# The state loops of four batches run back to back: batch ends and openings in pieces inside the loops

## The reference, cut to what matters

```
xz = x @ W_in.T;  u, z = split(xz)                  # 256 + 256 channels
uc = silu(conv3(u) + conv_b)                         # depthwise, along the tokens
proj = uc @ W_xproj.T;  B, C, dt = split(proj)       # 16, 16, 8
delta = softplus(dt @ W_dt.T + b_dt);  A = -exp(A_log)
h_t = exp(delta_t * A) * h_(t-1) + (delta_t * u_t) * B_t     # 16 states for each channel
y = sum_n(h * C) + uc * D
x = x + layernorm((y * silu(z)) @ W_out.T)
# experts: 8 of which the 2 best are weighted, and one shared, with gelu between two products
x = x + layernorm(sum_e combine_e * (gelu(x @ W1_e) @ W2_e) + shared(x))
```

## Time and profile before

| | us |
|---|---|
| median of 3 runs | 3171.16 (3161.33 to 3174.09) |
| profiled execution | 3168.89 |
| its span | 3166.6 |
| PE / DVE / ACT / POOL busy | 2388.2 / 2153.1 / 1719.2 / 1412.3 |
| granted PE clock, mean | 0.876 of full speed |

### The profile page before, as it was taken

How to read it: one execution, slowest core, us unless ns; L and a number is a source line. 1 busy time by engine, 2 the same in 40 slices (tenths; PEclk the granted TensorE clock), 3 DMA queues, 4 the chain that set the end, 5 groups by cost and what they waited for, 6 DMA issues and landing times.

```text
span 3166.6 us, 42245 instructions
## 1 busy us (share of the span) xinstructions
PE 2388.2 (75%) x15570; PEld 1726.5 (55%) x15570; DVE 2153.1 (68%) x3701; ACT 1719.2 (54%) x2617; POOL 1412.3 (45%) x1331
## 2 busy tenths in 40 slices
PE   3115772786377478699999999999999569876977
PEld 1003452354255356377777777776777446755675
DVE  3993897399569822588878887887888543355334
ACT  4213771675367233488877877787778323322332
POOL 0351143034204400256765676657656641564156
PEclk8556996799689789699999999999999879887988
DMA  3000000000000000100000000010000100000000
GB/s 99 0 0 0 1 1 0 1 1 1 0 0 1 1 1 6 49 21 21 21 21 21 21 21 21 21 31 21 21 22 10 41 1 1 1 13 2 1 1 14
DMA packets 32029, 42.02 MB, mean 13 GB/s; under 512 B 8897, under 2 KB 18130, under 8 KB 31442
## 3 DMA queue, kind: packets, MB, share of 16 engines
q1 hardware_dynamic: 31826, 39.34, 4.6%
HBM read 12.05 MB, written 2.10 MB: 4 GB/s over the span
## 4 chain that ended last, share of the span: by engine, by line
PE 46%; DVE 24%; issue 13%; POOL 10%; ACT 5%; SPq 1%; DMA 0%; POOLq 0%; DVEq 0%; ACTq 0%
PE ps L954 10%; PE ps L932 6%; PE ps L943 6%; PE ps L710 3%; DVE MA L1090 3%; DVE BIG L351 3%; PE ps L914 2%; PE ps L1723 2%; POOL MA L379 2%; DVE ps L340 2%; DVE BIG L340 2%; DVE lnb L265 2%; DVE acc L589 2%; PE ps L645 2%; PE ps L647 1%
## 5 line engine op out<-in xcount | busy, mean ns | idle before, releaser
L1090 DVE TENSOR_REDUCE MA<-ps 128x1 f32<-128x1024 f32 x512 | 623.4, 1221 | 192.9 <-PE ps L932 180.1
L379 POOL TENSOR_TENSOR MA<-MA,BIG 128x1024 f32<-128x1024 f32 x120 | 279.9, 2355 | 630.2 <-DVE BIG L351 630.2
L954 PE MATMUL ps<-MA,WB 128*64 128x128 f32 x4096 | 504.4, 277 | 0.0
L954 PEld LDWEIGHTS ps<-MA,WB 128*64 128x64 f32 x4096 | 442.6, 137 | 88.4 <-issue 87.4
L932 PE MATMUL ps<-BIG 96*128 96x512 f16 x1024 | 314.5, 389 | 13.4 <-ACT WB L1017 5.0
L710 PEld LDWEIGHTS ps<-WB,HR 128*128 128x128 f32 x2304 | 297.2, 204 | 26.5 <-issue 8.9
L1017 ACT ACTIVATE WB<-ps,MA 128x1024 f32<-128x1024 f32 x206 | 229.7, 1115 | 149.8 <-DVE MA L1090 149.8
L710 PE MATMUL ps<-WB,HR 128*128 128x128 f32 x2304 | 305.0, 289 | 0.0
L632 ACT ACTIVATE HR<-ps,b 128x512 f32<-128x512 f32 x288 | 190.8, 687 | 147.5 <-PE ps L647 146.7
L1024 ACT ACTIVATE MA<-ps 128x1024 f32<-128x1024 f32 x256 | 259.9, 1015 | 4.9 <-PE ps L943 4.9
L497 PE MATMUL ps<-bc,sel 96*128 96x512 bf16 x256 | 92.4, 451 | 198.5 <-DVE BIG L351 99.0
(11 more groups left out here) (291 smaller groups left out, 5310.9 us busy)
## 6 DMA issues: line engine op xcount, KB each, us to landing
BIG<-BIG SPq DMA_DIRECT2D x192, 64.0 KB, 2.0
BIG<-WB SPq DMA_DIRECT2D x192, 64.0 KB, 2.0
WB<-w_dram SPq DMA_DIRECT2D x1, 2304.0 KB, 14.5
X<-x_dram SPq DMA_DIRECT2D x4, 512.0 KB, 12.5
HR<-w_dram SPq DMA_DIRECT2D x1, 2048.0 KB, 9.3
out_dram<-X SPq DMA_DIRECT2D x4, 512.0 KB, 3.2
WB<-wqkv_dram SPq DMA_DIRECT2D x1, 1536.0 KB, 6.3
WB<-w_dram SPq DMA_DIRECT2D x2, 512.0 KB, 8.8
```

The source lines that it names most:

```text
L379: e.tensor_tensor(yy[:, c, :], yy[:, c, :], db[n % 2][c], ALU.add).then_inc(*p_my.up(b, n, c))
L954: x = e.matmul(bank[6][64 * pp:64 * pp + 64, 0:128], V[(4 * b + g) % 2][:, k, 64 * pp:64 * pp + 64], DT[n % 2][:, 128 * k:128 * k + 128], ...
L1090: e.tensor_reduce(L_of(n)[:, c:c + 1], ps[s][:, :], AX, ALU.max, negate=True).then_inc(*v_amx.up(n, s))
```

## The change

The opening of batch b+1, the end of batch b-1 and the experts of batch b-1 are given due times inside the loop of batch b, in slots of 14 between the states. For that:

- `up` is doubled, and delta is kept in it; `dl` as a tile of its own goes. The parts of the B and C rows get two buffers (`rows`), so that those of the next batch are made while this batch's are read. `du`, `uc`, `xT[0]` stay single.
- Everything of openings and ends that went through `ps[0]` and `ps[1]` goes through bank 7, in pieces of 512 tokens, one after another: two transposes, four products for u, two for `wx`, four for `wdt`, four for z, two for the output. Each piece waits until the copy of the piece before it has left the bank (`to`). For batch 0, banks 0, 1, 2, 3 and 7 are taken by turns.
- The down product of the experts has bank 6 alone in batches 0 to 2, and banks 6 and 7 in batch 3.
- `uc * D` is computed by ScalarE as the start of `yy`, and GpSimd adds all 16 states. The gate's product goes into `zs`, and the output product is copied by ScalarE into `lnb[0]` before statistics and normalisation. The projections are copied into the same SBUF tile and split from there. Convolution and softplus work in `lnb[0]`, `big[8]` and part of `BC`.
- The conversion of the first expert weights (`weights_act`, `weights_dve`) stands inside the opening of batch 0, no longer before it.

```diff
-M_AT = {"stats": 0, "norm": 3, "tr": 8, "in": 10, "conv": 17.2, "wx": 25.4, "bc": 29, "bc2": 31.2, "bc3": 33.2,
...
-M_PERIOD, N_PERIOD = 222, 9.4
+N_PERIOD, M_PERIOD, M_FIRST = 14.0, 224.0, 56.0
+def slot(n, more=9.5):
+    return N_PERIOD * n + more
+IN_AT = {"stats": slot(4), "norm": slot(5), "tr": 82.5, "u": 87, "conv0": slot(6), "conv1": slot(7), "silu": 111.5,
...
+OUT_AT = {"gate": slot(0), "yy": 12.2, "out": 12.5, "stats": slot(1), "rstd": 28.3, "norm": slot(2), "x": 42.3}
...
+        for i, p in enumerate(THROUGH):
+            x = bank[(0, 1, 2, 3, 7)[i % 5] if p[1] == 0 and p[0] in ("tr", "u", "wx", "wdt") else 0 if p == ("out", NB - 1, 1) else 7]
+            n = [k for k in range(8) if bank[k] is x][0]
+            path[p], user[n] = (x, user.get(n)), p
...
+        def loop_dve(e, b):
             for n in range(16):
                 k = n % 2
-                yield m_at(b, "n", N_PERIOD * n)
+                yield l_at(b, n)
                 e.wait_ge(*t_mrow[0].at(b, n))
...
+                for c in (1, 0):
+                    yield l_at(b, n, 2.4 if c else 4.7)
                     e.wait_ge(*a_mda.at(b, n, c))
...
+            for c in range(2):
+                yield in_at(b, f"conv{c}")
+                e.wait_ge(*a_m.at("u", b, c, 1))
...
+        def to(e, *p):
+            bk, last = path[p]
+            if last:
+                e.wait_ge(*a_m.at(*last))
+            return bk
...
+                    yield in_at(b, "u", (2 if b else 0.9) * (2 * c + h))
+                    bk = to(e, "u", b, c, h)
+                    e.wait_ge(*a_m.at("tr", b, h))
+                    e.matmul(bk, winT[:, 128 * c:128 * c + 128], xT[0][:, 512 * h:512 * h + 512], start=True,
+                             stop=True).then_inc(*t_m.up("u", b, c, h))
...
+        def down(b, k):
+            return bank[6 + k % 2] if b == NB - 1 else bank[6]
...
-            weave(over(mamba_dve, e), over(moe_dve, e))
+            weave(weights_dve(e), over(loop_dve, e), over(front_dve, e), over(back_dve, e), over(moe_dve, e))
```

More of the change, by code:

```diff
@@ L208, in const_pool @@
+        dl = [x[:, :, 1:1025] for x in up]
         def const_pool(e):
@@ new lines, in middle_act @@
+        def middle_act(e, b):
+            yield out_at(b - 1, "yy") if b else in_at(0, "du", 1)
+            for c in range(2):
+                if b:
+                    e.wait_ge(*v_mgate.at(b - 1, c))
+                e.activation(yy[:, c, :], uc[:, c, :], ACT.Identity, bias=0.0, scale=small["dcol"][:, c:c + 1]).then_inc(
+                    *a_myy.up(b, c))
+            for c in range(2):
+                for h in range(2):
+                    yield l_at(b, 0, 20.5 + 2 * (2 * c + h))
+                    e.wait_ge(*t_m.at("z", b, c, h))
+                    e.activation(zs[:, c, 512 * h:512 * h + 512], path["z", b, c, h][0], ACT.Silu, bias=0.0, scale=1.0).then_inc(
+                        *a_m.up("z", b, c, h))
@@ new lines, in back_act @@
+        def back_act(e, b):
+            for h in range(2):
+                yield out_at(b, "out", 2 + 2.5 * h)
+                e.wait_ge(*t_m.at("out", b, h))
+                if b + 1 < NB and h == 0:
+                    e.wait_ge(*v_mdl.at(b + 1, 1))
+                e.activation(lnb[0][:, 4 * h:4 * h + 4, :], path["out", b, h][0].rearrange("p (j c) -> p j c", j=4), ACT.Copy,
+                             scale=1.0).then_inc(*a_m.up("out", b, h))
+        def to(e, *p):
[3 more added lines that the diff above has]
+            return bk
@@ new lines, in middle_pe, with back_pe @@
+        def middle_pe(e, b):
+            for c in range(2):
+                for h in range(2):
+                    yield l_at(b, 0, 19.5 + 2 * (2 * c + h))
+                    bk = to(e, "z", b, c, h)
+                    e.matmul(bk, winT[:, 256 + 128 * c:384 + 128 * c], xT[0][:, 512 * h:512 * h + 512], start=True,
+                             stop=True).then_inc(*t_m.up("z", b, c, h))
+        def back_pe(e, b):
+            for h in range(2):
+                yield out_at(b, "out", 2.5 * h)
+                bk = to(e, "out", b, h)
+                for c in range(2):
+                    e.wait_ge(*v_mgate.at(b, c))
+                for j in range(4):
+                    t = 512 * h + 128 * j
+                    for c in range(2):
+                        i = e.matmul(bk[:, 128 * j:128 * j + 128], zs[:, c, t:t + 128], small["woT"][:, c, :],
+                                     start=c == 0, stop=c == 1)
+                i.then_inc(*t_m.up("out", b, h))
@@ L588, in moe_dve @@
                 for j in range(4):
-                    i = e.scalar_tensor_tensor(out=acc[:, 4 * h + j, :], in0=bank[6 + kk % 2][:, 128 * j:128 * j + 128],
+                    i = e.scalar_tensor_tensor(out=acc[:, 4 * h + j, :], in0=down(b, kk)[:, 128 * j:128 * j + 128],
                                                scalar=G6[:, 4 * h + j, x:x + 1], in1=acc[:, 4 * h + j, :], op0=ALU.mult,
```

539 lines of the change are left out of this document (279 added, 260 removed).

## The result

The changed kernel takes 3073.7 us (median of 4 runs, 3071.1 to 3076.8) against 3170.1 us before in the same session: ratio 0.970, 95% interval 0.968 to 0.972. Its profiled execution has a span of 3070.9 us. The prediction was 3039 us with a range of 2955 to 3105: direction and range hold, the size of the gain does not (96 us instead of 131).

The account below looks back on a forecast made before the run. The prediction took the loops as bound by VectorE and the pauses by a chain through all engines. Start, four loops and tail summed to 1133.8 us against 1264.1, 130.3 less, giving 3039 us, range 2955 to 3105.

Parts of the forecast that it names:

- start: Time to the first state loop: 74.3 us, 10.9 earlier, since batch 0's normalisation comes before the weight conversion.
- loop 0: First state loop: 16 states of 9.09 us, next batch's opening 26.4, eight lock places 27.2; 199.0 us.
- loop 1: Second state loop: VectorE's work 207.1 us, lock 30.6, a delayed scan 1.3, matmul waits 3.0; 242.0 us.
- loop 2: Third state loop: same as loop 1 plus 2.3 us where two output normalisations stand in a row; 244.3 us.
- loop 3: Last state loop: no opening in it, one lock place 3.4 us, 2.5 more for TensorE; 193.2 us.
- tail: From the last loop's end to the phase's end: grows by 9.5 us to 181.0, with 2.7 expert steps left.
- What bounds, and what the change can win: Loops bound by VectorE, pauses by a chain through all engines; only the pauses' idle part, some 64 us each, can be won.
- The lock: VectorE's SBUF pieces behind each state's two products meet GpSimd's two additions: 3.4 us at each of 27 places, 91.8 us.
- The waits: Loops 1 to 3: accumulation, down product and next accumulation chain through one PSUM bank, 3.0 us a loop.
- The single down bank shows in every step: Rival: in 51 expert steps the one-bank chain sticks out by 1.3 us, 66 us in all; 3105 us, chance 0.18.
- One wait or none: Rival: a piece waits for one of GpSimd's additions (2980 us) or for none (2947 us); chance 0.22.
- The slower case: Rival: bank 7 pieces hold TensorE's queue and the row products VectorE needs, 54 pieces of 4.9 us; 3304 us, chance 0.05.

Follow-up runs that it names:

- e8_weights_first: Changed kernel with the conversion of the expert weights put ahead of the first batch's opening again: 3082.0 us, ratio 0.973.
- e1_before_c: Changed kernel with VectorE's pieces just ahead of a state's two last products instead of behind them: 3053.1 us, ratio 0.965.
- e2_two_banks: Changed kernel with the third batch's down products, beside the last loop, alternating between two PSUM banks: 3068.8 us, ratio 0.970.
- e3_sparse: Changed kernel with one expert step a state in the last loop instead of 1.56: 3092.8 us, ratio 0.978.
- e4_exp: Changed kernel with exponential in place of gelu in the third batch's experts, so no table loads in the last loop: 3063.1 us, ratio 0.968.
- e12_fill: Changed kernel with 20 unread matmuls added in the last loop where TensorE waits 4.68 us for a gelu: 3060.2 us, ratio 0.969.
- e5_done_later: e1_before_c with the accumulations of batches 0 to 2 due later, 12.0 instead of 9.3 units: 3054.9 us, ratio 0.965.
- e9_light: Changed kernel with one of three matmuls of each up product left out in the experts of batches 0 to 2: 3061.5 us, ratio 0.969.

## Why the prediction was right, and where it was off

Each term of the sum beside its measurement; "busy" is VectorE's, "waits" is the rest of the loop.

| term | predicted busy + waits | measured busy + waits |
|---|---|---|
| start | 74.3 | 72.8 |
| loop 0 | 199.0 + 0 | 194.4 + 3.4 |
| loop 1 | 239.0 + 3.0 | 224.2 + 19.2 |
| loop 2 | 241.3 + 3.0 | 232.3 + 20.4 |
| loop 3 | 187.7 + 5.5 | 187.9 + 32.8 |
| tail | 181.0 | 181.3 |
| sum | 1133.8 | 1168.7 |

**What bounds, and what the change can win: right.** The pauses are gone, and the layer behind is unchanged.

**Start and tail: right** within 1.5 and 0.3 us, and e8_weights_first gives 9.9 us for the reordering that was priced at 10.9.

**The lock: right in kind, a quarter too dear.** Predicted were 27 places of 3.4 us, 91.8. The normalisation lost 3.2, the convolution 3.1; but the first convolution and the first cast of the rows found their data late from ScalarE (3.20 and 2.65 us of idle VectorE in loop 1), by which time the additions were over, or nearly so for the cast (1.51 us instead of 0.69), and the second softplus came behind them. About 69 us were lost, 2.6 a place. The Trainium skill, "SBUF — State Buffer", section "SBUF: two separate sides", gives the exclusive lock for a whole instruction; e1_before_c agrees with it. The 5.29 us of eight small operations show that the second addition takes the lock again: had they waited for the first addition alone, they would have ended near 133.0 us (half of 128.55 to 133.19, and 2.12 behind it), and they ended at 134.81.

**The waits: the step that failed.** The text had "3.0 a loop" for accumulation, down product and next accumulation in a chain through one bank, and 2.5 more in loop 3 for TensorE. Measured are 19.2, 20.4 and 32.8 us with 3.4 in loop 0: the forecast was 64 us too low, and 28 us too much for VectorE's work, most of it lock, hid a part. Of the 39.6 us in loops 1 and 2, 23.6 are the accumulations' and 11.7 are waits for what ScalarE copies out of bank 7 ahead of the convolution and the first cast. The prediction had these hand-overs at nothing, as hidden. That loops 1 and 2 came out within 1.4 and 8.4 us of the forecast is this cancelling, not precision. In loop 3 the bank had nothing to do with it (e2_two_banks); for loops 1 and 2 no run tried a second bank, and the trace has 3.2 us of TensorE's waiting for it in each. What the runs show in its place, for loop 3: the density of expert steps (e3_sparse, 13 us of idle time), the table loads (e4_exp, 5 to 7 us of the loop), and a clock that falls behind a gap in TensorE's work (e12_fill, 7 to 9). They overlap and don't add up. For loops 1 and 2 the runs exclude VectorE's own work (e1_before_c), the accumulations' place (e5_done_later) and most of TensorE's work (e9_light); that TensorE and VectorE hold each other up in their rows remains. The 122 us in which TensorE's row products wait for VectorE speak for it, but it is not shown by an edit of its own. Half-clock stretches like that of loop 3 stand in these loops (at 460 to 474 and 713 to 727 us); filling the gaps ahead of them was not tried. The longer ones (301 to 355, 546 to 598 and 799 to 847 us) leave VectorE about 0.5 us idle each, so the loops don't lose there.

**The rivals.** "The single down bank shows in every step" named the right symptom, idle VectorE before accumulations, and a time (3105) that is 31 us too high where the forecast is 35 too low; its cause is excluded in loop 3 and not shown elsewhere. "One wait or none" is excluded by the 5.29 us; the mean place, 2.6 us, lies between one wait (1.2) and the 3.4 of the forecast. The slower case did not come: in loops 1 to 3 row products made VectorE wait once, 4.5 us.

The fastest version with the whole computation is e1_before_c, 3053.1 us, about 20 us under the changed kernel; e5_done_later is the same within the noise.

## What to carry to other kernels

When two engines with orders of their own hand work back and forth, count idle time from the coupling as a term of its own; here it was 19 to 33 us a loop where 3 to 5.5 were forecast. A stall that is removed from one of them may come back for the greater part as waiting: of 56 us here the phase kept 20. Put VectorE's SBUF work where GpSimd is idle, which one number did here. And look at TensorE's granted clock right behind its gaps: here a wait of 4.68 us cost another 7 to 9.

## What was not expected of the hardware

More work made a loop shorter: 20 matmuls that nobody reads, 4.5 us, kept TensorE's clock at its upper level and took 7 to 9 us off. And the clock fell at the same place of the order whether TensorE had waited 4.68 us (the changed kernel) or 1.83 us (e4_exp) just before.
